# A graph layer's last normalisation moved into TensorE's products, with every third residual sum on ScalarE and GpSimd

## The chip, the cores and the metric

The kernel runs on one core of one Trainium2 chip. The metric is the device time of one execution in microseconds (us). Three executions of the kernel before took 1694.15, 1694.95 and 1696.44 us; their median is 1694.95 us.

## What is computed

A graph convolution layer on 6250 nodes with 256 channels and 100,000 edges, then a feed-forward layer with 8 experts of which each node takes one. Cut to the part that matters here, the end of the graph layer and what comes right behind it:

```python
edge_index = jnp.stack([src, dst])
# inside the graph layer, x is the layernorm of the input
h = _gcn_conv(x, W1, row, col, n_nodes)
h = jax.nn.relu(_batchnorm(h, g1, b1))
h = _gcn_conv(h, W2, row, col, n_nodes)      # 256 channels
h = _batchnorm(h, g2, b2)                    # per channel: h * a2 + b2
out = jax.nn.relu(h + res)                   # res = x
# around it
x = x + _L0_gnn_ref(_layernorm(x, axis=-1), edge_index, ...)
x = x + _L0_ffn_ref(_layernorm(x, axis=-1)[None], ...)[0]
```

So each node's row becomes x + relu(h * a2 + b2 + layernorm(x)), and that row is normalised once more (mean and variance over 256 channels) for the feed-forward layer.

## The kernel before, in words

The work goes through stages one after the other: edges are sorted into one-hot matrices, the first aggregation, the two linear maps, the second aggregation (to 1209 us of the profile), the end of the graph layer (`finish_gnn`), the gate with the hidden units (`gate`), and the experts. The change touches `finish_gnn` alone. It has no barrier to the gate: its five functions (`sync`, `gpsimd`, `vector`, `scalar`, `tensor`) are the first part of each engine's program in the gate's block, and each engine works in the order in which its instructions are written.

The nodes are cut into 49 tiles of 128 rows. Two tiles are a pair (25 pairs, the last with one tile) and four a group (13 groups, the last with one tile). A pair fills one of four PSUM banks, `m.ps[:, g % 4]`. The second convolution lies in `m.agg2` with the channels on the partitions, in two halves (KC = 2), so a tile has to be turned.

- SP (`sync`, L1563 and L1566) loads, for each group, 512 KB of x into `xr` and 512 KB of the stored layernorm(x), as two f16 parts, into `xnr`. Both are rings of 12 tiles, that is three groups. Group q + 3 is loaded once both pairs of group q have been summed (`s_x1`, L1571).
- DVE first makes the per-channel factors a2 and b2 (L1593 to L1602, the power on GpSimd at L1583).
- ScalarE (`affine`, L1662) applies a2 and b2 to `m.agg2` in place, two instructions of 128x512 for a group. It does four groups ahead, and then in turn: `normalise(q)` (L1669, four instructions of 128x256) and `affine(q + 4)`.
- TensorE (L1693, L1695) makes, for each tile, the sum in PSUM: two products of the identity with the f16 parts (256 columns each), then two fp32 products that turn the two halves of `m.agg2` by the identity `m.id32`. Each fp32 product is two instructions in the trace. It waits for the load, for the bank (`s_x1` of the pair four before) and for `s_v`, that is `affine` of the group. After the pairs 16 and 18 it turns the first two normalised pairs for the gate (L2024).
- DVE (`residual`, L1611) takes the pair out of PSUM: max with 0 plus x, to `m.rows`, 128x512. `stats` (L1619) takes the statistics of the pair before, and at the end of a group come L1625 and L1627; GpSimd raises to the power -0.5 (L1587), and `shifts(q)` (L1639) runs in DVE's step g = 2q + 4. So in a step DVE does residual(g), stats(g - 1), and in every second one the end of a group and a shift. In step 22 it does the gate's L2164 twice, in step 23 the gate's weights (L1631 to L1633).
- ScalarE's `normalise(q)` waits for that shift. Behind the last one it loads the table of Gelu and starts the gate (L2106).

## Time and profile before

| | |
|---|---|
| median of 3 executions | 1694.95 us |
| profiled execution, its own time | 1694.88 us |
| its span, first to last instruction | 1693.2 us |
| mean granted TensorE clock | 0.978 of full speed |
| `finish_gnn`, from SP's first load to TensorE's first hidden unit | 1209.42 to 1264.30 us |
| first Gelu of the gate | 1271.32 us |

The page of the profile gives busy shares over the whole span, which mix eight stages with different limits. For this change only the stretch from 1209 to 1272 us is read, by four views: the busy time of each engine in a stretch, the chain of work that ended last in order of time, the timeline of the instructions, and the groups of instructions by line with the time of one.

### The profile page before, as it was taken

The page shows a single profiled execution, that of the slowest core. Times are in us where ns is not written, and L with a number is a line of the kernel's source. Part 1 is how long each engine was busy: PE and PEld are TensorE (multiplying, and loading weights), DVE is VectorE, ACT ScalarE, POOL GpSimd, SP SyncE. Part 2 cuts the span into 40 slices and gives each one's busy share as a digit, 9 for nine tenths or more (in the row PEclk, how much of TensorE's full clock was granted, in tenths as well). Part 3 has the DMA queues.
Part 4 walks back from the last instruction along what each step waited for, and adds up shares of the span by engine and source line. Part 5 has one row for each costly group of instructions (what it writes and reads, how often), then busy time and mean ns, then how long its engine had stood idle before and what let it go on. Part 6 is the DMA issues. An engine that isn't in the chain of part 4 may idle for free. (4 is left out here: it accounts for less than half of the span.)

```text
span 1693.2 us, 32733 instructions
## 1 busy us (share of the span) xinstructions
PE 1473.3 (87%) x10003; PEld 1028.2 (61%) x10004; DVE 1091.2 (64%) x3900; ACT 851.7 (50%) x1611; POOL 1036.8 (61%) x1139
## 2 busy tenths in 40 slices
PE   0137999999999989798999999999779999839998
PEld 0114666666666669796665555556566666627776
DVE  6578888888888737683233343433386778767775
ACT  0555555555555535574234432221288877725665
POOL 5745677777777710244777777777223566637776
PEclk9999999999999999899999999999899999959999
DMA  7727666666666620046989999998489433489993
GB/s 242 203 90 258 200 201 208 203 206 211 200 209 210 203 61 0 23 163 230 324 286 313 316 311 324 329 324 277 139 279 343 162 152 151 164 212 262 271 271 87
DMA packets 219570, 364.80 MB, mean 215 GB/s; under 512 B 31416, under 2 KB 146551, under 8 KB 219174
## 3 DMA queue, kind: packets, MB, share of 16 engines
q1 hardware_dynamic: 158202, 217.62, 39.2%
q0 software_dynamic: 46816, 131.61, 24.7%
q10 hardware_dynamic: 14412, 13.86, 3.2%
q8 instruction: 69, 1.13, 0.3%
q14 instruction: 71, 0.58, 0.1%
HBM read 240.34 MB, written 130.12 MB: 219 GB/s over the span
## 5 line engine op out<-in xcount | busy, mean ns | idle before, releaser
L1181 POOL DMA_INDIRECT grows<-table_dram,gsrc x680 | 656.4, 965 | 248.3 <-issue 214.9
L1113 PE MATMUL ps<-table,adj 128*128 128x512 f16 x2842 | 705.0, 380 | 4.2 <-PEq L1330 4.2
L1113 PEld LDWEIGHTS ps<-table,adj 128*128 128x128 f16 x2842 | 389.5, 142 | 165.1 <-issue 6.8
L857 ACT ACTIVATE adj<-ps 128x490 f16<-128x490 f32 (+1 forms) x390 | 223.9, 574 | 179.5 <-PE ps L842 174.8
L829 DVE TENSOR_SCALAR oh_k<-iota_k,keyrem 128x246 f16<-128x246 f16 x780 | 237.1, 308 | 0.0
L828 DVE TENSOR_SCALAR oh_r<-iota_r,keyrem 128x128 f16<-128x128 f16 x780 | 211.9, 273 | 4.1 <-ACT keyrem L352 3.7
L1062 PE MATMUL ps<-grows,oh_g 128*128 128x512 f16 x680 | 166.5, 379 | 18.1 <-DMA grows<-table_dram,gsrc 17.8
L2395 PE MATMUL ps<-wd,h_hi 128*128 x896 | 152.7, 276 | 15.3 <-DVE h_lo L2443 15.3
L842 PE MATMUL ps<-oh_k,oh_r 128*128 128x245 f16 x780 | 148.8, 273 | 17.3 <-DVE oh_k L829 13.6
L842 PEld LDWEIGHTS ps<-oh_k,oh_r 128*128 128x128 f16 x780 | 75.7, 99 | 95.1 <-DVE oh_k L829 19.9
L934 DVE SCALAR_TENSOR_TENSOR tmp_d<-ps,disP,tmp_d 128x256 f32<-128x256 f32 x30 | 14.5, 484 | 183.6 <-ACT tmp_d L1140 183.6
L927 DVE TENSOR_SCALAR oh_g<-iota_r,gloc 128x128 f16<-128x128 f16 x680 | 124.8, 277 | 0.3 <-DVE cv_raw L806 0.2
L2395 PE MATMUL ps<-wd,h_lo 128*128 x448 | 123.2, 275 | 0.0
L1062 PEld LDWEIGHTS ps<-grows,oh_g 128*128 128x128 f16 x680 | 64.7, 98 | 94.9 <-DMA grows<-table_dram,gsrc 27.6
L2038 PE MATMUL ps<-q_xt_hi,fw_parts 128*128 128x512 f16 (+1 forms) x416 | 102.4, 368 | 5.0 <-DVE wg L1633 3.1
L1148 ACT ACTIVATE agg<-ps 128x256 f32<-128x256 f32 x98 | 37.4, 382 | 135.7 <-PE ps L1074 104.9
L2395 PEld LDWEIGHTS ps<-wd,h_hi 128*128 128x128 f16 x896 | 84.4, 99 | 32.2 <-issue 15.6
L2375 POOL DMA_INDIRECT out<-out_rows,token x56 | 75.4, 1346 | 46.5 <-POOL out_rows L2372 40.7
L2106 ACT ACTIVATE q_hf<-ps,b1f,unscale 128x512 f32<-128x512 f32 (+1 forms) x104 | 78.4, 754 | 41.2 <-PE ps L2038 37.9
L2175 DVE SCALAR_TENSOR_TENSOR q_h_lo<-q_hf,beta,q_h_hi 128x512 f16<-128x512 f32 (+1 forms) x104 | 74.6, 718 | 36.3 <-ACT q_h_hi L2117 34.4
L1140 ACT ACTIVATE tmp_d<-ps,disP 128x256 f32<-128x256 f32 x30 | 14.2, 474 | 159.8 <-PE ps L1113 159.8
L2443 DVE TENSOR_TENSOR h_lo<-back,h_hi 128x1024 f16<-128x1024 f32 x56 | 68.9, 1230 | 39.6 <-ACT h_hi L2412 39.5
(379 smaller groups left out, 2709.4 us busy)
## 6 DMA issues: line engine op xcount, KB each, us to landing
kept<-sorted_h SPq DMA_DIRECT2D x224, 128.0 KB
adj_dram<-adj SPq DMA_DIRECT2D x60, 367.5 KB
adj<-adj_dram SPq DMA_DIRECT2D x56, 367.5 KB, 7.5
cv_raw<-fwd SPq DMA_DIRECT2D x64, 256.0 KB, 6.7
adj_dram<-adj SPq DMA_DIRECT2D x30, 477.8 KB
adj<-adj_dram SPq DMA_DIRECT2D x28, 477.8 KB, 5.5
table_dram<-table SPq DMA_DIRECT2D x13, 896.0 KB, 4.1
grows<-table_dram,gsrc POOLq DMA_INDIRECT x680
```

What stands on the lines that cost most here:

```text
L828: dve.tensor_scalar(a.oh_r[:, n % OHR, i, :], m.iota_r[:, :], m.keyrem[:, 1, j, w:w + 1], None, ALU.is_equal)
L829: last = dve.tensor_scalar(a.oh_k[:, n % OHR, i, :], m.iota_k[:, :], m.keyrem[:, 0, j, w:w + 1], None, ALU.is_equal)
L842: last = pe.matmul(m.ps[:, n % 3, at:at + keys], a.oh_r[:, n % OHR, i, :], a.oh_k[:, n % OHR, i, 0:keys], start=True, stop=True)
L857: act.activation(m.adj[:, q % 3, d0:d0 + wide, :].rearrange("r d c -> r (d c)"), m.ps[:, n % 3, 0:wide * NT], ACT.Copy).then_inc(a.s_adj, 1)
L927: last = dve.tensor_scalar(m.oh_g[:, n % GOR, j, :], m.iota_r[:, :], m.gloc[:, g, part * BT + j:part * BT + j + 1], None, ALU.is_equal)
L1062: last = pe.matmul(acc, m.oh_g[:, n % GOR, j, :], m.grows[:, n % GR, j, :], start=False, stop=part == PT - 1 and j == PARTS[part] - 1)
L1113: last = pe.matmul(acc, adj[:, :, c], table[:, c, :], start=c == 0, stop=c == NT - 1)
L1181: pool.indirect_dma_start(m.grows[:, n % GR, j, :], None, m.table_dram, bass.IndirectOffsetOnAxis(ap=m.gsrc[:, g, part * BT + j:part * BT ...
L2038: last = pe.matmul(m.ps[:, c % UB, 0:wide], m.w1[:, 2 * k + half, w, at:at + P], x[:, i % 2, k, 0:wide], start=q == 0 and k == 0, stop=q = ...
L2106: act.activation(hf[:, c % HFR, 0:wide], m.ps[:, c % UB, 0:wide], ACT.Gelu, bias=m.b1f[:, h:h + 1], scale=m.unscale[:, 0:1]).then_inc(s_ge ...
L2375: pool.indirect_dma_start(a.out, bass.IndirectOffsetOnAxis(ap=token[:, q:q + 1], axis=0), outt[:, q % HB, :], None, bounds_check=N - 1, oo ...
L2395: last = pe.matmul(acc, h[:, q % HB, c, :], w[:, c // 2, half, c % 2, :], start=False, stop=h is h_lo and c == KH - 1)
```

## The change

- ScalarE no longer applies a2 and b2. DVE makes two diagonal matrices of a2 (`dg`), and TensorE turns with `dg[:, h, :]` in place of `m.id32`, so that the turned tile is scaled.
- b2 is added by one more product: a matrix `two` of 1/32 (64x128, float32r) with `shift2` (64x256, float32r), which holds a high part of b2's row in 32 partitions and the rest in the other 32. To get b2 as a row, DVE first fills `dg` with diagonals of b2, TensorE sums them over the partitions with `m.ones` into bank 7, and DVE copies that (64x256) and subtracts to get the rest. One wait `s_v` stands before the shift product of pair 0.
- The products are issued for a pair: two of 512 columns in place of four of 256, and one shift product of 512 columns.
- In the pairs 2, 5, 8, 11, 14, 17 and 20 (`aside`) the sum isn't DVE's: ScalarE takes the relu out of PSUM (`bare`, 128x512), GpSimd adds x (`add`, 128x512 fp32) and signals `s_added`. `stats` of such a pair, and the reload of its ring slot, wait for `s_added`; TensorE waits for `s_bare` before it uses the bank again. ScalarE does bare(g) for g in 2q + 4 and 2q + 5 before normalise(q); GpSimd does add(g) for g in 2q + 2 and 2q + 3 before the power of group q.

```diff
@@ -1549,11 +1549,20 @@
     s_ve, s_mh, s_rs, s_aff, s_v, s_sum = (S("g_" + n) for n in ("ve", "mh", "rs", "aff", "v", "sum"))
     s_h, s_x1, s_ve3, s_rs3, s_shift3, s_wg = (S("g_" + n) for n in ("h", "x1", "ve3", "rs3", "shift3", "wg"))
     s_in = [S(f"g_in{q}") for q in range(RG)]
+    s_bare, s_added = S("g_bare"), S("g_added")
     pairs = [(2 * g, min(2, NT - 2 * g)) for g in range(-(-NT // 2))]
     groups = [(GT * q, min(GT, NT - GT * q)) for q in range(-(-NT // GT))]
     done = [-(-(t0 + k) // 2) for t0, k in groups]
+    aside = [g for g in range(2, len(pairs) - 3, 3)]
+    shared = lambda n: sum(g < n for g in aside)
+    own = lambda n: n - shared(n)
     gw = m.gw
     m.s_normed = S("g_normed")
+    dg = take("dg", [P, KC, P], F32)
+    shift2 = take("shift2", [64, C], F32R)
+    two = take("two", [64, P], F32R)
+    s_wide = S("g_wide")
+    WIDE = 7
     assert take.next <= m.work + 6144
     def sync(sp):
         def load(q):
@@ -1568,7 +1577,9 @@
         for q in range(RG):
             load(q)
         for q in range(len(groups) - RG):
-            sp.wait_ge(s_x1, done[q])
+            sp.wait_ge(s_x1, own(done[q]))
+            if shared(done[q]):
+                sp.wait_ge(s_added, shared(done[q]))
             load(q + RG)
             if q == 3:
                 sp.dma_start(gw.wg_raw[:, :, :], a.fwg.rearrange("(k p) e -> p k e", p=P)).then_inc(gw.s_par, 16)
@@ -1581,8 +1592,21 @@
         pool.wait_ge(s_mh, 1)
         pool.wait_ge(s_ve, 1)
         pool.tensor_tensor(rs2[:, :], ve2[:, :], mh[:, :KC], ALU.pow).then_inc(s_rs, 1)
+
+        def add(g):
+            t0, k = pairs[g]
+            q = t0 // GT
+            at = t0 % RT
+            v = m.rows[:, t0:t0 + k, 0:C]
+            pool.wait_ge(s_in[q % RG], 32 * (q // RG + 1))
+            pool.wait_ge(s_bare, shared(g) + 1)
+            pool.tensor_tensor(v, v, xr[:, at:at + k, :], ALU.add).then_inc(s_added, 1)
+
         for q, (t0, k) in enumerate(groups):
             t = slice(t0, t0 + k)
+            for g in range(2 * q + 2 if q else 0, 2 * q + 4):
+                if g in aside:
+                    add(g)
             pool.wait_ge(s_ve3, q + 1)
             pool.tensor_tensor(rs3[:, t], ve3[:, t], mh[:, t], ALU.pow).then_inc(s_rs3, 1)
             if q in beside:
@@ -1599,10 +1623,22 @@
         dve.wait_ge(s_rs, 1)
         link(dve.tensor_tensor(a2[:, :], m.bn_g2[:, :], rs2[:, :], ALU.mult))
         link(dve.tensor_tensor(tmp[:, :], mv2[:, :, 0], a2[:, :], ALU.mult))
-        dve.tensor_tensor(b2[:, :], m.bn_b2[:, :], tmp[:, :], ALU.subtract).then_inc(s_aff, 1)
+        link(dve.tensor_tensor(b2[:, :], m.bn_b2[:, :], tmp[:, :], ALU.subtract))
+        for h in range(KC):
+            last = dve.tensor_scalar(dg[:, h, :], m.id32[:, :], b2[:, h:h + 1], None, ALU.mult)
+        last.then_inc(s_aff, 1)
+        dve.tensor_scalar(two[:, :], m.ones[0:64, :], 1.0 / 32, None, ALU.mult)
+        dve.wait_ge(s_wide, 1)
+        for h in range(KC):
+            dve.tensor_scalar(dg[:, h, :], m.id32[:, :], a2[:, h:h + 1], None, ALU.mult)
+        low = slice(32, 64)
+        link(dve.tensor_copy(shift2[:, :], m.ps[0:64, WIDE, 0:C]))
+        dve.tensor_tensor(shift2[low, :], m.ps[low, WIDE, 0:C], shift2[low, :].bitcast(F32), ALU.subtract).then_inc(s_v, 1)
 
         def residual(g):
 
+            if g in aside:
+                return
             t0, k = pairs[g]
             q = t0 // GT
             at = t0 % RT
@@ -1614,7 +1650,10 @@
         def stats(g):
             t0, k = pairs[g]
             q = t0 // GT
-            dve.wait_ge(s_x1, g + 1)
+            if g in aside:
+                dve.wait_ge(s_added, shared(g) + 1)
+            else:
+                dve.wait_ge(s_x1, own(g) + 1)
             for i in range(t0, t0 + k):
                 dve.bn_stats(st3[:, i, :], m.rows[:, i, 0:C]).then_inc(s_sum, 1)
             if t0 + k == sum(groups[q]):
@@ -1655,51 +1694,56 @@
         dve.tensor_copy(m.rows[:, :, C + 2], mv3[:, :, 0])
 
     def scalar(act, beside):
-        def affine(q):
-            t0, k = groups[q]
-            for h in range(KC):
-                v = m.agg2[:, h, t0 * P:(t0 + k) * P]
-                last = act.activation(v, v, ACT.Identity, bias=b2[:, h:h + 1], scale=a2[:, h:h + 1])
-            last.then_inc(s_v, 1)
-
         def normalise(q):
             t0, k = groups[q]
             act.wait_ge(s_shift3, q + 1)
             for i in range(t0, t0 + k):
                 act.activation(m.rows[:, i, 0:C], m.rows[:, i, 0:C], ACT.Identity, bias=shift3[:, i:i + 1], scale=rs3[:, i:i + 1]).then_inc(m.s_normed, 1)
 
-        act.wait_ge(s_aff, 1)
-        AHEAD = 4
-        for q in range(AHEAD):
-            affine(q)
+        def bare(g):
+            t0, k = pairs[g]
+            act.wait_ge(s_h, g + 1)
+            act.activation(m.rows[:, t0:t0 + k, 0:C], m.ps[:, g % 4, 0:k * C].rearrange("p (t c) -> p t c", c=C), ACT.Relu).then_inc(s_bare, 1)
+
         for q in range(len(groups)):
+            for g in range(2 * q + 4 if q else 0, 2 * q + 6):
+                if g in aside:
+                    bare(g)
             normalise(q)
             if q in beside:
                 beside[q]()
-            if q + AHEAD < len(groups):
-                affine(q + AHEAD)
 
     def tensor(pe, beside):
+        pe.wait_ge(s_aff, 1)
+        for h in range(KC):
+            last = pe.matmul(m.ps[:, WIDE, h * P:(h + 1) * P], m.ones[:, :], dg[:, h, :], start=True, stop=True)
+        last.then_inc(s_wide, 1)
         for g, (t0, k) in enumerate(pairs):
             q = t0 // GT
             if t0 % GT == 0:
                 pe.wait_ge(s_in[q % RG], 32 * (q // RG + 1))
             if g >= 4:
-                pe.wait_ge(s_x1, g - 3)
-            pe.wait_ge(s_v, q + 1)
+                pe.wait_ge(s_x1, own(g - 3))
+                if shared(g - 3):
+                    pe.wait_ge(s_bare, shared(g - 3))
+            at = t0 % RT
+            for n in range(2):
+                pe.matmul(m.ps[:, g % 4, 0:k * C], m.id16[:, :], xnr[:, at:at + k, n * C:(n + 1) * C], start=n == 0, stop=False)
+            if g == 0:
+                pe.wait_ge(s_v, 1)
+            pe.matmul(m.ps[:, g % 4, 0:k * C], two[:, :], shift2[:, :].unsqueeze(1).to_broadcast([64, k, C]), start=False, stop=False)
             for i in range(k):
                 acc = m.ps[:, g % 4, i * C:(i + 1) * C]
-                for n in range(2):
-                    pe.matmul(acc, m.id16[:, :], xnr[:, (t0 + i) % RT, n * C:(n + 1) * C], start=n == 0, stop=False)
                 for h in range(KC):
-                    last = pe.matmul(acc[:, h * P:(h + 1) * P], m.agg2[:, h, (t0 + i) * P:(t0 + i + 1) * P], m.id32[:, :],
-                                     start=False, stop=h == KC - 1)
+                    last = pe.matmul(acc[:, h * P:(h + 1) * P], m.agg2[:, h, (t0 + i) * P:(t0 + i + 1) * P], dg[:, h, :],
+                                     start=False, stop=i == k - 1 and h == KC - 1)
             last.then_inc(s_h, 1)
             if g in beside:
                 beside[g]()
         pe.wait_ge(s_wg, 1)
         pe.wait_ge(gw.s_w1, 16)
-        pe.wait_ge(s_x1, len(pairs))
+        pe.wait_ge(s_x1, own(len(pairs)))
+        pe.wait_ge(s_added, len(aside))
 
     lead = Names()
     lead.sync, lead.gpsimd, lead.vector, lead.scalar, lead.tensor = sync, gpsimd, vector, scalar, tensor
```

## Rows read from the trace of the kernel before

**Rows 1.** Busy time by stretch: us, each engine's busy time, clock, DMA share, GB/s.
```profile
1236.00:1246.00 10.00, 7.34 (x65) 6.65 (x64) 9.08 (x35) 9.65 (x18) 2.77 (x3) 1.00 0.89 281
```
**Rows 2.** Chain that ended last, in order of time: start us, us, what.
```profile
1234.33 0.16 DVE shift L1639
1234.52 2.07 ACT rows L1669 x4
1236.59 1.42 ACT agg L1662 x2
...
1239.74 0.69 DVE rows L1611
...
1241.12 0.39 DVE mv L1625 x4
1241.61 0.16 DVE shift L1639
...
1258.65 0.69 DVE rows L1611
...
1265.47 4.53 ACT rows L1669 x9
```
**Rows 3.** Timeline, start of the stage: start, us, engine, line, what.
```profile
1214.26 0.16 DVE L1602 TENSOR_TENSOR b2c<-bn_b,tmp 128x2 f32<-128x2 f32 x1
...
1216.49 1.06 PE L1695 MATMUL ps<-id,agg 128*128 128x128 f32 x4
...
1218.95 0.69 DVE L1611 SCALAR_TENSOR_TENSOR rows<-ps,x_ring 128x512 f32<-128x512 f32 x1 [4.53 <-PE ps L1695]
```
**Rows 4.** Timeline, TensorE, one tile at full clock, and the next tile.
```profile
1238.80 0.38 PE L1693 MATMUL ps<-xn_ring,id 128*128 128x256 f16 x2
...
1239.47 0.38 PE L1693 MATMUL ps<-xn_ring,id 128*128 128x256 f16 x2
```
**Rows 5.** Chain in the gate's stage: six f16 products of 512 columns.
```profile
1277.89 1.31 PE ps L2038 x6
```
**Rows 6.** Timeline, linear stage, TensorE: float32r products of 256 columns, start to start.
```profile
721.77 0.64 PE L1530 MATMUL ps<-w_hi,h_hi 128*128 128x256 f32 x4
722.25 0.64 PE L1530 MATMUL ps<-w_lo,h_hi 128*128 128x256 f32 x4
```
**Rows 7.** One line: the float32r product of 64 rows, 256 columns, durations.
```profile
L2391 PE MATMUL ps<-bd_rows,ones_r x56: 375/380/572, 1495.7 to 1683.9; 64*128 x56
```
**Rows 8.** Groups by line: busy us, mean ns: GpSimd adds of two widths, ScalarE's evacuation.
```profile
L2372 POOL TENSOR_TENSOR out_rows<-part_rows,x_rows 128x256 f32<-128x256 f32 x56 | 42.2, 754 | 17.3 <-ACT part_rows L2423 17.1
...
L1348 POOL TENSOR_TENSOR w_lo<-w_raw,w_hi 128x1024 fp32r<-128x1024 f32 x1 | 2.4, 2367 | 0.1
...
L2125 ACT ACTIVATE turned<-ps x52: 277/587/599, 1278.0 to 1484.9; 128x512 f32<-128x512 f32 x48, 128x128 f32<-128x128 f32 x4
```
**Rows 9.** Issue of one group's loads, and the landing of single loads of xn_ring.
```profile
1238.57 0.37 SPq L1563 DMA_DIRECT2D x_ring<-x  x1
1238.98 0.51 SPq L1566 DMA_DIRECT2D xn_ring<-xn_dram  x1
...
DMA to landing us min/median/max: 4.9/4.9/4.9
...
DMA to landing us min/median/max: 6.0/6.0/6.0
```
**Rows 10.** Groups by line, DVE: small operations like those added.
```profile
L2275 DVE TENSOR_SCALAR bd_parts<-bd,g_up 64x256 fp32r<-64x256 f32 x1 | 0.3, 345 | 0.0
```
**Rows 11.** Timeline, linear stage: DVE with and without GpSimd beside it.
```profile
727.97 0.68 DVE L1422 TENSOR_TENSOR h_lo<-h_all,h_hi 128x512 fp32r<-128x512 f32 x1
...
728.97 1.29 POOL L1361 CAST h_hi<-h_all 128x512 fp32r x2 [1.30 <-ACT h_all L1474]
729.33 0.48 DVE L1426 SCALAR_TENSOR_TENSOR table<-ps,dis,table 128x256 f32 x1 [0.69 <-ACT table L1479]
729.73 1.06 DVE L1422 TENSOR_TENSOR h_lo<-h_all,h_hi 128x512 fp32r<-128x512 f32 x1
```

## The prediction, made before the changed kernel was run

> **What bounds the kernel now.** I read the busy times by stretch first. In ten steady microseconds of the stage ScalarE is busy for 9.65 us, DVE for 9.08 and TensorE for 7.34 [rows 1]. Two engines are close to full and neither is quite, so I went to the chain of work in order of time. It shows a circle: a shift on DVE at 1234.33, four instructions of normalise (2.07 us), two of affine (1.42), a pair on TensorE, the residual at 1239.74, statistics, the end of a group, and the shift two groups on at 1241.61 [rows 2]. That circle of 7.28 us carries four pairs: 1.82 us a pair. ScalarE's own work in it is 2 x (2.07 + 1.42) = 7.0 us, so ScalarE is nearly the bound and the waits around it are the rest. The last part matters as well: residual(22) starts at 1258.65, and what follows it (steps 22 to 24 on DVE, nine instructions of normalise for 4.53 us, Gelu's table) leads to the first Gelu [rows 2]. From there the gate and the experts run as they did. So the time is the profiled 1694.88 us plus the shift of residual(22). The profiled execution stands 0.07 us under the median of 1694.95.
>
> **What goes.** The 26 instructions of affine leave ScalarE, 2 x 0.71 us a group by the chain [rows 2], some 17 us in all, and with them the circle. Seven of 25 residuals leave DVE. Every remaining product has to be made by engines that had slack, so the question is what is late next.
>
> **The start.** b2 is ready at 1214.26 + 0.16 = 1214.4 [rows 3]. Before, affine of group 0 followed, and residual(0) started at 1218.95 [rows 3]. Now two diagonals of 128x128 come first. No row has just that; the nearest is 0.345 us for 64x256 [rows 10], the half of it is 0.17 for 128 columns, and I take 0.2 each (bounds 0.1 and 0.35): 1214.9. TensorE's two fp32 sums are four instructions at half clock, 1.06 us for four [rows 3]: 1216.0. DVE then makes two diagonals (0.4), the copy of 64x256 (0.35), and the subtraction (0.35 to 0.5) [rows 10]: about 1217.3. TensorE's two f16 products are done by then. The shift product and eight fp32 instructions at half clock are twice 0.24 and twice 0.88 (below), 2.2 us, and with 0.2 to the signal pair 0 is complete at 1219.7. So residual(0) starts 0.75 us later than it did. After that I let TensorE run at full clock, as before, where it had risen to it by then.
>
> **TensorE for a pair.** Before: a tile takes 1239.47 - 1238.80 = 0.67 us, 0.22 for the two f16 products and 0.45 for four fp32 instructions [rows 4], so 1.33 a pair. Now: two f16 products of 512 columns, 1.31 / 6 = 0.218 each [rows 5]; eight fp32 instructions, the same form as before, 0.88; and the shift product. Four float32r products of 256 columns start 0.48 apart [rows 6], 0.12 each, so 0.24 for 512 columns. The one with 64 rows shows 0.380 us from start to end [rows 7], which holds its fill and its weights; twice that less nothing is the upper bound, 0.76, and 0.11 (half of an f16 one) the lower. I take 0.24, since [rows 6] are a dense stream, as this is. Sum: 0.44 + 0.24 + 0.88 = 1.55 us a pair, 0.22 more than before. TensorE alone, from pair 0 at 1219.7, would complete pair 22 after 22 x 1.55 + 0.9 for the gate's turned pairs, at 1254.7. That is 4 us before 1258.65: TensorE isn't the bound yet.
>
> **DVE.** From the residual at 1239.74 to the end of its step's statistics at 1241.12 are 1.38 us, and a group's end with the shift takes 0.49 to 0.65 more [rows 2]. Four pairs without waiting cost 4 x 1.38 + 2 x 0.57 = 6.7 of the 7.28 us. With a third of the residuals gone, each 0.69 [rows 2], it is (6.7 - 0.9) / 4 = 1.45 a pair: under TensorE's 1.55. DVE isn't the bound either, whatever the sums aside save it.
>
> **The path through a pair that is put aside.** ScalarE takes the relu out of PSUM: 0.587 us for 128x512 [rows 8]. GpSimd's add of 128x512 has no row. The nearest are 0.754 us for 256 columns and 2.367 for 1024 [rows 8]; between them 512 columns lie at 1.29, which I take, with 0.75 and 2.37 as ends. So a pair put aside is summed about 0.1 + 0.59 + 1.29 = 2.0 us after TensorE, where DVE needs 0.7. Its statistics stand one step later on DVE, 1.55 + 0.69 = 2.2 us after, so they just fit. But its ring slot also comes free later. For the pairs 5, 11 and 17, each the second of its group, SP's wait on `s_added` is what releases the group three on; behind it SP's queue holds all later loads.
>
> **The loop that decides.** From add(5) to add(11): issue of x, 0.03 + 0.41 us until that of xn; its landing, in six steady loads 4.9 three times, then 5.0, 5.8 and 6.0, mean 5.25 (the ends in [rows 9]); pairs 10 and 11 on TensorE, 3.10 and 0.2 to the signal; relu 0.59; add 1.29. Sum 10.87 us for six pairs: 1.81 a pair, where the old circle had 1.82 [rows 2]. The removed bound is replaced by an equal one. Placing it: pair 5 completes at 1219.7 + 5 x 1.55 = 1227.45; add(5) ends at 1229.4; two laps give 1251.1 for add(17). Then issue 0.44, landing 5.25, pair 22 at 1.55, signal 0.2: residual(22) can start at 1258.6, against 1258.65. The sum is a change of 0.0 us, and 1695.0 us.
>
> Its ends: landing always 4.9 makes three loads 1.0 us faster, always 6.0 makes them 2.3 slower (the DMA share is already 0.89 [rows 1], so crowded loads are likelier than free ones); the add at 0.75 gives -1.6, at 2.37 gives +3.2 (three adds in the chain); the shift product at 0.76 would add 0.5 to each of ten pairs, +5, at 0.11 takes 1.3 off; the diagonals' bounds move the start by -0.4 to +0.6. Two extremes at once in the same direction are unlikely. SP's load of the hidden units' weights stands behind these waits too, but it moves with them by under 2 us, and TensorE waits for DVE's L1633 then.
>
> Is the add a risk to DVE? While GpSimd's cast ran, DVE's instruction with two SBUF inputs took 1.06 us in place of 0.68, and the one that reads PSUM kept its 0.48 [rows 11]. DVE's residual reads PSUM and one ring, the statistics one tensor, so I cost the sharing at nothing; if each of seven adds cost DVE 0.38, that is 2.7 us in an engine with slack, under 1 at the end. The Trainium skill (GPSIMD Engine Reference, 1. Specifications) says that GpSimd's SBUF interface is shared with VectorE, with contention for instructions that have two SBUF inputs or use a two-port mode: by that rule the residual is spared too, and the trace agrees with it. The same page (3.1 Elementwise) calls GpSimd the wrong engine for plain elementwise work and gives 2.6 cycles an element at 1.2 GHz, an estimate of 1.11 us for this add; with it the sum would be 0.5 us lower.
>
> **The rivals.**
> 1. The loads don't hold the stage. If the landings stay at 4.9 us and the add is nearer to 1.0, the chain drops under TensorE's own pace. Then TensorE and DVE in their order set it: residual(22) between 1254.7 (TensorE alone) and about 1255.5 with DVE's waits, so 3.2 to 4.0 us gained: 1691.3. For it: the transfers have gaps, share 0.89. Against: TensorE's waits are then all gone, which needs every load on time. Chance 0.13.
> 2. Slower: the ring slot's late release. If the add takes over 1.9 us beside DVE's traffic, or loads that are issued closer together than before land in 6.0, each lap grows by 1.0 to 1.4 us and nothing gives it back: 3 x 1.3 = +4, 1699. It decides from a lap over 12.0 us. For it: the DMA share, and that two of the six landings were near 6. Against: the narrow add's 0.754 was steady in 56 of them. Chance 0.15.
> 3. The change doesn't do what it says: the shift product isn't cheap (0.76), so TensorE takes 2.07 a pair and is the bound from start to end: 1219.7 + 22 x 2.07 + 0.9 = 1266.1, 7.5 us later: 1702.5. Only the isolated product [rows 7] speaks for it, the dense stream against it [rows 6]. Chance 0.03.
>
> **How the numbers follow.** The forecast, no change within the spread of landings, has 0.69. A measurement here tells apart about 0.2%, 3.4 us. Rival 1 lies at that bound, so 0.11 of its chance and of the forecast's low tail counts as faster; rival 2 and 3 give 0.17 slower; 0.72 within. The range leaves out a tenth on each side: 1691.8 to 1698.8.
>
> **What would show it right or wrong.** Right: no L1662; TensorE's pairs 1.55 apart when it doesn't wait; it waits for the loads of groups 5, 8 and 11, over 1 us each; SP's longest waits end by GpSimd's add; add(11) to add(17) near 10.9 us; ScalarE under 75% busy. Wrong: if TensorE waits for nothing between pairs 6 and 22 (rival 1), if the adds take over 1.9 us or the lap over 12 (rival 2), if pairs on TensorE are 2 us apart (rival 3), or if the first Gelu moves otherwise than residual(22) does.

## The result, and the profile of the changed kernel

| | before | after |
|---|---|---|
| median of six executions each | 1694.55 us (1691.45 to 1696.44) | 1701.03 us (1699.92 to 1702.71) |
| ratio, 95% interval | | 1.0041 (1.0031 to 1.0051) |
| profiled execution, its own time | 1694.88 us | 1700.47 us |
| mean granted TensorE clock | 0.978 | 0.976 |
| first load of the stage to residual(0) | 9.53 us | 11.04 us |
| first load to residual(22) | 49.23 us | 56.54 us |
| first load to first Gelu | 61.90 us | 69.20 us |
| first Gelu to the end of the span | 421.9 us | 421.6 us |

The changed kernel is 6.5 us slower, outside the forecast range (1691.8 to 1698.8). The table's lower half is read from the timelines: the whole loss stands before residual(22), 1.5 us in the start and 5.8 us in the 22 pairs between, and the first Gelu moved with it (+7.3). Behind the first Gelu the two agree within 0.3 us. The two spans differ by less, 5.4 us (1698.6 and 1693.2), because the changed kernel's profile reached this stage 1.6 us sooner, by stages that the change doesn't touch. So the question is about 46 us of this one stage. The marks come from one profile each; they are finer than whole times, since executions of one kernel differ by 2 or 3 us elsewhere.

The busy times of the ten microseconds that answer to [rows 1] (columns as there):

```profile
1236.00:1246.00 10.00, 9.67 (x56) 6.33 (x55) 6.32 (x30) 5.12 (x11) 4.49 (x4) 1.00 0.82 245
```

ScalarE fell from 9.65 to 5.12 and DVE from 9.08 to 6.32, as meant. TensorE rose from 7.34 to 9.67: it is the bound. From 1237.9 us to the residual of pair 22 the chain of work in order of time has nothing else in it (start us, us, what):

```profile
1232.36 5.51 DMA xn_ring<-xn_dram
...
1247.82 0.43 PE ps L1731 x2
1248.25 0.42 PE ps L1734
1248.67 1.09 PE ps L1738 x8
1249.76 0.43 PE ps L1731 x2
...
1263.17 1.10 PE ps L1738 x8
...
1264.36 0.69 DVE rows L1647
```

A pair takes 1249.76 - 1247.82 = 1.94 us where the forecast had 1.55. The timeline of TensorE and of its weight loads (PEld) shows where it goes; the brackets hold the idle time ahead of a row:

```profile
1227.70 0.59 PE L1731 MATMUL ps<-xn_ring,id 128*128 128x512 f16 x2
1228.22 0.50 PE L1734 MATMUL ps<-shift,two 64*128 64x512 f32 x1
1228.65 1.16 PE L1738 MATMUL ps<-dg,agg 128*128 128x128 f32 x8
1229.65 0.60 PE L1731 MATMUL ps<-xn_ring,id 128*128 128x512 f16 x2
...
1228.22 0.18 PEld L1734 LDWEIGHTS ps<-shift,two 64*128 64x128 f32 x1 [0.42 <-issue]
1228.65 0.97 PEld L1738 LDWEIGHTS ps<-dg,agg 128*128 128x128 f32 x8 [0.25 <-issue]
```

From start to start: 0.52 us for the two f16 products, 0.43 for the shift product, 1.00 for the eight fp32 instructions, 1.95 in all. The load of the 64-row weights starts at the very moment of its product, 1228.22, after 0.42 us in which the loader did nothing, and the load of the next 128-row weights starts with its product too, after 0.25 us. The waits by reason, from 1216 to 1264 us, say the same of the whole stage (total us, times, longest):

```profile
DVE rows L1647 <- PE ps L1738: 17.1, 13, 3.0
PEld ps L1734 <- issue: 9.7, 22, 0.8
PEld ps L1738 <- issue: 6.0, 23, 0.4
PE ps L1731 <- DMA xn_ring<-xn_dram: 0.3, 1, 0.3
```

DVE waits for TensorE 13 times, and TensorE waits for a load once, for 0.3 us. That is the load of group 5 at the head of the chain above; the relu and the add of pair 5 released it. So the loop on which the forecast rested is touched once and costs 0.3 us; it doesn't set the pace.

The start of the stage, in the timeline:

```profile
1212.85 0.48 DVE L1628 TENSOR_SCALAR dg<-id,b2c 128x128 f32<-128x128 f32 x2
1213.38 1.22 PE L1719 MATMUL ps<-dg,ones 128*128 128x128 f32 x4 [7.64 <-DVE dg L1628]
1215.48 0.42 DVE L1636 TENSOR_TENSOR shift<-ps,shift 32x256 fp32r<-32x256 f32 x1
1216.68 2.08 PE L1738 MATMUL ps<-dg,agg 128*128 128x128 f32 x8
1218.54 1.06 PE L1731 MATMUL ps<-xn_ring,id 128*128 128x512 f16 x2
...
1221.86 0.59 PE L1731 MATMUL ps<-xn_ring,id 128*128 128x512 f16 x2
```

Pair 1 runs from 1218.54 to 1221.86, 3.32 us, nearly all of it at half clock (the lower of the clock's two levels, 1.2 GHz): in the busy times by stretch TensorE's granted clock is 0.50 from 1219 to 1221, 11.2 to 13.2 us behind the first load, and 0.86 in the next two. Before, it was 0.85 already 9.6 to 11.6 us behind it.

With that the loss closes. Between residual(0) and residual(22) lie 22 pairs at 1.945 (42.8), 1.38 more for pair 1, two turned pairs of the gate at 0.44 (0.9) and 0.3 of waiting: 45.4, and the trace has 56.54 - 11.04 = 45.5.

### The profile page after: what moved, and what is told of

It reads as the page before. It is cut to its first block and busy times, and to the rows that moved or that the text cites. A ratio compares the mean times of both kernels' runs of the same rounds, so it can differ in the third digit from the quotient of the medians.

```text
span 1698.6 us, 32690 instructions
## 1 busy us (share of the span) xinstructions
PE 1491.4 (88%) x9984; PEld 1029.7 (61%) x9985; DVE 1088.3 (64%) x3900; ACT 837.3 (49%) x1592; POOL 1044.4 (61%) x1146
## 3 DMA queue, kind: packets, MB, share of 16 engines
q8 instruction: 68, 1.11, 0.3%
```

## The experiments

The theory before the first run was that the shift product's 64 rows cost, or its type, or both; the rivals were the sums put aside and the products for pairs. The short marks below are us behind the stage's first load. The chips of e5, e6, e8 and e9 took some 2000 us for every kernel, those of e9b, e6b, e10 and e7 some 1974. There the stage began at 1470 to 1502 us instead of 1206 to 1210. Its own rows agree: e5's stage repeats that of the changed kernel, and the stored layernorm's loads land after 4.8 to 5.8 us in e7 and 4.9 to 6.0 in before. So the marks of all runs are set side by side. How finely they can be read is shown by e3, e6, e6b, e9 to e12 and e14 to e16, which run the same instructions up to pair 1: their residual(1) lies anywhere from 11.85 to 13.02 us, since the clock rises at another moment in each, 11.0 us behind the first load in e3 and 11.7 in e15. Differences of about 1 us between two rows are therefore not read as effects.

| run | residual(0) | residual(22) | first Gelu | median, and kernel before on the same chip | ratio (95%) |
|---|---|---|---|---|---|
| before | 9.53 | 49.23 | 61.90 | | |
| after | 11.04 | 56.54 | 69.20 | 1701.03 / 1694.55 | 1.0041 (1.0031 to 1.0051) |
| e1 float32r, 128 rows | 10.76 | 50.86 | 63.52 | 1699.70 / 1694.35 | 1.0034 (1.0021 to 1.0047) |
| e2 f16, 64 rows | 10.87 | 53.71 | 66.37 | 1698.54 / 1694.35 | 1.0029 (1.0019 to 1.0038) |
| e3 f16, 128 rows | 10.58 | 50.59 | 63.24 | 1695.88 / 1694.35 | 1.0009 (1.0001 to 1.0018) |
| e4 no shift product | 10.33 | 49.93 | 62.59 | 1697.10 / 1694.35 | 1.0011 (1.0000 to 1.0022) |
| e5 after, no pair aside | 11.06 | 56.48 | 69.13 | 2011.3 / 2003.94 | 1.0051 (1.0021 to 1.0082) |
| e6 e3, no pair aside | 10.57 | 49.05 | 61.70 | 2003.93 / 2003.94 | 1.0009 (0.9985 to 1.0033) |
| e6b the same | 10.58 | 49.48 | 62.12 | 1974.33 / 1973.74 | 0.9987 (0.9952 to 1.0022) |
| e8 before, pairs aside | 9.53 | 52.52 | 65.17 | 2009.82 / 2003.94 | 1.0023 (0.9996 to 1.0051) |
| e7 before, products for pairs | 9.53 | 49.94 | 62.60 | 1975.85 / 1973.74 | 1.0006 (0.9981 to 1.0031) |
| e9 e3, first pair of five groups aside | 10.59 | 52.30 | 64.95 | 2000.88 / 2003.94 | 0.9994 (0.9969 to 1.0018) |
| e9b the same | 10.58 | 52.50 | 65.14 | 1971.87 / 1973.74 | 0.9990 (0.9956 to 1.0024) |
| e10 e3, first pair of ten groups aside | 10.58 | 52.44 | 65.07 | 1977.91 / 1973.74 | 1.0017 (0.9979 to 1.0054) |
| e11 e3, half-height loads | 10.57 | 50.95 | 63.62 | 1695.60 / 1694.71 | 1.0008 (0.9994 to 1.0023) |
| e14 e9, half-height loads | 10.38 | 49.41 | 62.05 | 1695.23 / 1694.71 | 1.0002 (0.9992 to 1.0011) |
| e12 e6, half-height loads | 10.31 | 49.77 | 62.42 | 1694.85 / 1694.71 | 1.0003 (0.9993 to 1.0013) |
| e13 before, half-height loads | 9.52 | 50.86 | 63.53 | 1694.61 / 1694.71 | 1.0001 (0.9991 to 1.0010) |
| e15 e3, x alone loaded | 10.58 | 47.50 | 60.14 | 1691.88 / 1693.91 | 0.9989 (0.9979 to 0.9998) |
| e16 e9, x alone loaded | 10.45 | 47.71 | 60.35 | 1692.34 / 1693.91 | 0.9990 (0.9980 to 0.9999) |

**Height and type of the shift product (e1, e2, e3).** e1 fills both operands to 128 rows, the upper half of `two` with zeros; e2 keeps 64 rows in f16; e3 does both.

```diff
-    shift2 = take("shift2", [64, C], F32R)
-    two = take("two", [64, P], F32R)
+    shift2 = take("shift2", [P, C], F32R)      # e2: [64, C], F16; e3: [P, C], F16
+    two = take("two", [P, P], F32R)            # e2: [64, P], F16; e3: [P, P], F16
...
+        dve.tensor_scalar(two[64:P, :], m.ones[64:P, :], 0.0, None, ALU.mult)   # e1, e3
```

> The changed kernel with a shift product of 128 rows in place of 64: the two matrices get 128 partitions, the lower 64 rows of the weights are zero. Same type (float32r), same columns, same sum. Theory height: the trace of the changed kernel shows TensorE's pairs 1.94 us apart, not 1.55, and before the 64-row weights and again before the 128-row weights behind them the weight load starts only when the product before has nearly ended; a change of the rows in use stops the load from running ahead. Then here the pairs that don't wait are 1.55 to 1.62 us apart, and the loop of load, relu and add that I had predicted sets the pace: 1694 to 1697 us. Theory type: float32r of 512 columns, or its 4-byte weights, costs 0.43 us as such. Then the pairs stay at 1.9 and the time at 1701.

> The changed kernel with the shift product in f16 (high part and rest of b2's row in f16, weights f16), still of 64 rows. Theory height: nothing is gained, pairs 1.85 to 1.95 us apart, 1700 to 1701 us. Theory type: pairs at 1.55 to 1.6, and 1694 to 1697 us.

> The changed kernel with the shift product in f16 and of 128 rows. Both theories expect pairs of 1.52 to 1.58 us. What it tells: my prediction's loop (load of a ring slot, two pairs, relu on ScalarE, add on GpSimd: 1.81 us a pair) as the next bound expects 1694 to 1697 us, with TensorE waiting over 1 us for the loads of groups 5, 8 and 11. If TensorE's pace is all that matters, 22 pairs at 1.53 in place of 1.94 give 9 us: 1692.

Height is the cause. With 128 rows residual(22) comes at 50.86 and 50.59, with 64 rows at 56.54 and 53.71. The type is worth 2.8 us with 64 rows, and with 128 rows 0.3, which can't be told from nothing. Some of this is the clock's: residual(1) follows residual(0) by 3.27 us in the changed kernel, 2.20 in e1, 2.45 in e2 and 1.87 in e3, and whether the height delays the clock's rise or only its scatter shows here stays open. A pair of e1 on TensorE, and the load of the same weights:

```profile
1254.31 0.60 PE L1732 MATMUL ps<-xn_ring,id 128*128 128x512 f16 x2 [0.59 <-DMA xn_ring<-xn_dram]
1254.57 0.58 PE L1735 MATMUL ps<-shift,two 128*128 128x512 f32 x1
1254.98 1.05 PE L1739 MATMUL ps<-dg,agg 128*128 128x128 f32 x8
1255.88 0.59 PE L1732 MATMUL ps<-xn_ring,id 128*128 128x512 f16 x2
...
1254.54 0.19 PEld L1735 LDWEIGHTS ps<-shift,two 128*128 128x128 f32 x1
```

The pair takes 1255.88 - 1254.31 = 1.57 us, and the weights' row has no idle time ahead of it any more. The f16 product of 64 rows in e2 still has both idle times:

```profile
1253.00 0.39 PE L1734 MATMUL ps<-shift,two 64*128 64x512 f16 x1
1253.32 1.16 PE L1738 MATMUL ps<-dg,agg 128*128 128x128 f32 x8
...
1254.84 0.09 PEld L1734 LDWEIGHTS ps<-shift,two 64*128 64x128 f16 x1 [0.42 <-issue]
1255.16 0.97 PEld L1738 LDWEIGHTS ps<-dg,agg 128*128 128x128 f32 x8 [0.23 <-issue]
```

Its pair takes 1.84. What the type still saves is the exposed load itself, 0.09 us against 0.18. So in these traces the weights of 64 rows aren't loaded while products of 128 rows run, nor the other way round, and each change of height lays the end of one product and the next load bare: 1.94 - 1.57 = 0.37 us a pair in float32r, 1.84 - 1.54 = 0.30 in f16 (e3's pairs stand 1.54 apart).

The Trainium skill (TensorEngine Tiling (Array Packing), Key Properties) says that a change of tiling mode, not just of the tile, drains TensorE. The idle 0.42 and 0.25 us would agree with that, if a plain product of 64 rows is such a change; whether it is this rule that acts, no run here shows.

In whole times the height shows between e2 (1.0019 to 1.0038) and e3 (1.0001 to 1.0018), not between the changed kernel and e1. e1's five executions spread from 1695.83 to 1702.00 us, and their median, 1699.70, misses the 1694 to 1697 that were expected. Its profile is that of the lowest, so the marks speak for that one; why others took longer is open. e2 took 1698.54 us and 1.84 a pair, where the height alone was expected to leave 1700 to 1701 and 1.85 to 1.95; e3's time came as expected.

**The price in place (e4).** The shift product is left out, so b2 is missing from the sum.

```diff
-            pe.matmul(m.ps[:, g % 4, 0:k * C], two[:, :], shift2[:, :].unsqueeze(1).to_broadcast([64, k, C]), start=False, stop=False)
```

> The changed kernel without the shift product in the pairs; b2's row is still made, but not added, so that part of the computation is missing. TensorE's pair would take 0.44 + 0.88 = 1.32 us. The predicted loop without the shift product is (0.44 + 5.25 + 2.64 + 0.2 + 0.59 + 1.27) / 6 = 1.73 us a pair, 1693 to 1695 us. If the loads land in time whatever the pace, DVE's 1.45 a pair is the bound: 1690 to 1691. Its difference to the changed kernel is the whole price of the shift product where it stands: 6 to 8 us by the loop, 10 by DVE.

The shift product of the changed kernel cost 69.20 - 62.59 = 6.6 us at the first Gelu, as the loop had it (6 to 8); that of e3 only 0.65, less than the marks can tell. So in e3 TensorE's work isn't the bound any more. The medians show less: 1701.03 against 1697.10, 3.9 us, and e4's misses its expected 1693 to 1695. Its executions spread from 1691.7 to 1700.0, with 1694.65 for the profiled one.

**The sums put aside (e5, e6, e8).** e5 takes them out of the changed kernel and e6 out of e3; e8 adds them alone to the kernel before, where ScalarE still applies a2 and b2.

```diff
-    aside = [g for g in range(2, len(pairs) - 3, 3)]
+    aside = []
...
-        pe.wait_ge(s_added, len(aside))
```

> The changed kernel (shift product float32r of 64 rows) with no pair put aside: DVE takes all 25 residuals, ScalarE and GpSimd sum none. If TensorE's 1.94 us a pair is the bound in the changed kernel, the third of the sums on other engines neither helps nor harms: DVE needs 1.67 a pair, residual(22) starts within 0.5 us of where it did after the stage's start (56.5 us) and the time is 1700 to 1702. If the pairs put aside were what slowed the changed kernel, it would be 1696 to 1698.

> The f16 shift product of 128 rows, and no pair put aside. DVE's work without waiting is 1.67 us a pair, the ring's loop without relu and add (0.44 + 5.25 + 3.1 + 0.2 + 0.7) / 6 = 1.61, TensorE 1.55. If the late release of ring slots through add(5), add(11) and add(17) holds the kernel with this product and pairs aside (its residual(22) starts 50.6 us after the stage's start, with 3.6 us of waits for loads), this one is faster by 22 x 0.1 to 0.14 = 2 to 3 us at that point, at 47.5 to 48.5, and the time 1692 to 1694. If not, it is slower, since DVE has more to do.

> The kernel before with one part of the change alone: the pairs 2, 5, 8, ... 20 summed by ScalarE and GpSimd; a2 and b2 are still applied by ScalarE. ScalarE's work becomes 2 x 3.49 + 1.33 x 0.59 = 7.8 us for four pairs, over the circle's 7.28, and relu stands ahead of normalise and affine in its order: 1.94 us a pair, residual(22) 2 to 4 us later, 1697 to 1698. By the other view (DVE's work is the bound, ScalarE's waits are slack) it would be 2 us faster.

Under the 64-row product the sums do nothing: 56.48 without and 56.54 with them. Behind e3 they cost 1.1 to 1.5 us. On the kernel before they cost 3.3. Its chain there:

```profile
1532.40 0.07 DVE shift L1663
1532.50 2.08 ACT rows L1693 x4
1534.58 1.41 ACT agg L1686 x2
1535.99 1.97 ACT rows L1693 x4
1537.95 1.41 ACT agg L1686 x2
1539.36 0.49 ACT rows L1698
...
1539.99 1.29 POOL rows L1598
...
1543.92 0.07 DVE shift L1663
```

Normalise, affine and the relu (L1698) stand behind one another without a gap, and the add and the statistics behind them, up to the next shift: 11.52 us from shift to shift for six pairs, 1.92 a pair where the old circle had 1.82 and 1.94 was expected. So the relu and the add have both entered the circle. e6 missed its expectation, 47.5 to 48.5, by 0.6 us, and e6b, the same kernel, lies 1.0 above it; they come back to the old 49.23 and no further.

**What bounds e3.** With the price gone, the loop of the forecast is there, in its own order:

```profile
1226.75 1.29 POOL rows L1603
...
1228.10 0.37 SPq L1572
...
1228.52 5.75 DMA xn_ring<-xn_dram
...
1234.32 0.60 PE ps L1732 x2
...
1237.60 0.61 ACT rows L1707
...
1238.34 1.28 POOL rows L1603
...
1240.10 4.89 DMA xn_ring<-xn_dram
```

From the end of add(5), 1228.04, to the end of add(11), 1239.62, it is 11.6 us for six pairs, where the forecast had 10.87; the landing was 5.75 instead of 5.25, and the two pairs, the first after a wait, 3.26 instead of 3.10. The next lap, to the end of add(17) at 1250.78, took 11.2. TensorE waits 1.62, 1.06 and 0.72 us for the loads of groups 5, 8 and 11, where over 1 us each was expected.

**Other pairs aside (e9, e9b, e10).** If the late release by the second pair of a group holds the loop, taking the first pair of a group aside should free it.

```diff
-    aside = [g for g in range(2, len(pairs) - 3, 3)]
+    aside = [g for g in range(2, len(pairs) - 3, 4)]      # e10: step 2
```

> The f16 shift product of 128 rows, with the pairs 2, 6, 10, 14 and 18 put aside in place of 2, 5, 8, ... 20: all of them the first pair of their group, so that a ring slot is released by DVE's residual of the second pair. By the loop theory the release is no longer late: (0.44 + 5.25 + 3.1 + 0.2 + 0.7) / 6 = 1.61 us a pair, DVE 1.49, TensorE 1.55: residual(22) at 46.5 to 48 us after the stage's start, 1690.5 to 1693. If the place of the pairs in their groups doesn't matter, it stays near 50, 1695.

> The kernel of e9 once more, on another chip, since all kernels there took 2000 us with longer stages before this one. Loop theory: residual(22) at 46.5 to 48 us after the stage's start. The first look had 49.1 with a gap of 5 us between two residuals; if that gap comes again, the theory lacks something.

> The kernel of e6 (f16 shift product of 128 rows, no pair put aside) once more on another chip. The first Gelu came 61.7 us after the stage's start there, against 63.2 with the pairs put aside (e3). Loop theory: again 61 to 62 us, and a time of 1693 to 1695. If the other chip had disturbed the stage, it would lie elsewhere.

> The f16 shift product of 128 rows, and the first pair of every group put aside (2, 4, ... 20: ten pairs). DVE's work is 1.32 us a pair, the ring's release stays with DVE: loop 1.61, TensorE 1.55. Loop theory: as e9b within 0.5 us, the relief of DVE brings nothing more. If DVE's work were the bound in e9b, this one would be 1 to 3 us earlier.

All three came out at 52.3 to 52.5, later than e3, where earlier was expected; e6b's first Gelu, at 62.12, was about as expected. The timeline of e9b shows a late load and what it brought:

```profile
1518.84 0.60 PE L1732 MATMUL ps<-xn_ring,id 128*128 128x512 f16 x2 [2.18 <-DMA xn_ring<-xn_dram]
...
1519.50 1.83 PE L1739 MATMUL ps<-dg,agg 128*128 128x128 f32 x8
1521.12 1.06 PE L2069 MATMUL ps<-id,rows 128*128 128x128 f32 x4
1521.97 1.06 PE L1732 MATMUL ps<-xn_ring,id 128*128 128x512 f16 x2
```

and its busy time by stretch:

```profile
1518.00:1522.00 4.00, 3.16 (x16) 2.84 (x17) 1.32 (x3) 0.77 (x2) 1.05 (x2) 0.70 1.01 333
```

One load, issued while the share of the DMA engines' time stood at 0.95 to 1.10, landed after 7.4 us. TensorE waited 2.18 us for it, and soon after that idle time its granted clock fell to the lower of its two levels: eight fp32 instructions took 1.83 us instead of 1.05, the f16 pair of products 1.06 instead of 0.60, and the clock's mean over 1518 to 1522 is 0.70. The same instructions, from that load to the first fp32 one of the next pair, took 4.29 us here (to 1523.13) and 2.63 in e3 (1245.04 to 1247.67). So 1.7 us are the clock's, nearly all of the 1.9 by which e9b is later than e3. The waits aren't longer in sum, 3.3 us for loads against e3's 3.6, but two of them make it up. e9 and e10 show the same, a fall of the clock behind waits of 2.12 and 2.53 us. The length of the wait doesn't decide it alone: behind 2.64 us in e4 and 2.06 in e8 the clock stayed up.

**The transfers (e11 to e16).** Two ways of taking bytes away. In e11 to e14 only 64 of the 128 partitions of `xnr` are loaded from group 3 on; the other rows are stale. In e15 and e16 the stored layernorm isn't loaded again, but for the last group, and x comes in two halves to keep the count of the semaphore, so the bytes are halved over all partitions. The lines are cut:

```diff
+            rows = P if q < RG else P // 2                  # e11 to e14
+                sp.dma_start(xr[:, at + b:at + b + 2, :], ...).then_inc(s_in[q % RG], 16)   # e15, e16: b = 0 and 2, no xnr
```

> The kernel of e3 (f16 shift product of 128 rows, every third pair aside) with less to load: from group 3 on only 64 of the 128 partitions of the stored layernorm are loaded, 256 KB in place of 512, so half of these rows of the sum are stale and that part of the computation is wrong. TensorE, DVE, ScalarE and GpSimd do the same instructions. In e3 the stage loses 3.6 us in waits for loads. Loop theory: landing about 0.9 us earlier, three of them in the chain: residual(22) 2.5 to 3.5 us earlier than in e3 (50.6 after the stage's start), at 47 to 48. If only the late release by relu and add mattered and not the transfer, it would stay at 50 or above.

> The kernel of e9 (first pairs of groups aside) with the same halved load. In e9 the loads landed up to 7.4 us after their issue, at a DMA share of 0.96, and residual(22) came at 52.4. Transfer theory: the DMA queue was full; now landings are back at 4 to 5 us and residual(22) comes at 46 to 47.5, earlier than in any kernel so far. If something else in the order of this kernel holds it (a wait of statistics for the add), it stays over 50.

> The kernel of e6 (f16 shift product of 128 rows, no pair aside) with the halved load. Its residual(22) came at 49.1 and 49.5 with 2 us of waits for loads. If DVE's 1.67 us a pair is its bound, it gains those waits at most: 47 to 48.5. If the transfer is, as in e14: 46 to 47.

> The kernel before with the halved load. My reading of its chain is that ScalarE's circle of normalise and affine sets the pace and the loads are in time: residual(22) stays within 0.5 us of 49.2. If the load is the hidden bound of the kernel before too, it comes 2 us earlier.

None of the four came where it was expected (e11 only where it would stay if the transfer didn't matter), and they settle little. Half the bytes over half the partitions landed no sooner: 5.41, 5.63 and 6.61 us in e11's chain against 4.89, 4.93 and 5.75 in e3's, and the kernel before got 1.6 us later by it. Only e14 says something: where e9's clock fell its own stays at 1.00, and residual(22) comes 2.9 us earlier, of which some 1.7 are the clock's, going by e9b.

> The kernel of e3 with the stored layernorm loaded for the first three groups and the last only; the other groups load x alone, in two transfers of 256 KB over all 128 partitions, and TensorE adds a stale layernorm, which is the part of the computation that is wrong. The load over 64 partitions (e11) landed 5.4 to 6.6 us after its issue, no sooner than a full one, so e11 didn't test the transfer; this does. Transfer theory: landing 3.5 to 4.2 us after the first issue in place of 5.3 to 6.7, so the loop is (0.03 + 4 + 3.1 + 0.2 + 0.59 + 1.27) / 6 = 1.53 us a pair, no more than TensorE's 1.54: residual(22) 45.5 to 47.5 us after the stage's start, in place of 50.6. If the late release by relu and add is the whole of it, 50 to 51 again.

> The kernel of e9 (first pairs of groups 2, 6, ... 18 aside) with the loads of e15. Transfer theory: residual(22) at 45 to 47, within 1 us of e15, though these two lay 1.8 us apart with full loads (50.6 and 52.4); both are then at TensorE's pace (10.6 + 22 x 1.54 + 0.9 = 45.4). If e16 stays over 49, the place of the pairs aside has a cost of its own that isn't the transfer.

e15 came at 47.50, the upper end of what was expected. e16 missed its 45 to 47 with 47.71, but lies within the expected 1 us of e15. Busy times of e15, then of e16, in its steady stretch:

```profile
1223.00:1253.00 30.00, 29.44 (x215) 24.33 (x214) 27.22 (x104) 20.24 (x40) 16.62 (x15) 1.00 0.54 160
```
```profile
1225.00:1255.00 30.00, 29.41 (x212) 24.05 (x210) 25.14 (x97) 19.39 (x38) 14.66 (x14) 1.00 0.50 152
```

With a DMA share of 0.54 TensorE is busy for 29.44 of 30 us, from pair 1 on 18 of its 23 steps are 1.53 or 1.54 us, and residual(22) comes at 47.50, 3.1 us before e3's; e16 gains 4.8 on e9b, 1.7 of them the clock's, and ends at the same place. So the transfers hold e3 and e9. With them out of the way it makes no difference which pairs are put aside, at least at TensorE's pace, where both now stand. Whether one of the two orders would be the faster one ahead of a quicker TensorE, these runs can't show.

**The products for pairs (e7).** The kernel before, with the two f16 products of 512 columns alone.

```diff
-                for n in range(2):
-                    pe.matmul(acc, m.id16[:, :], xnr[:, (t0 + i) % RT, n * C:(n + 1) * C], start=n == 0, stop=False)
...
+            for n in range(2):
+                pe.matmul(m.ps[:, g % 4, 0:k * C], m.id16[:, :], xnr[:, at:at + k, n * C:(n + 1) * C], start=n == 0, stop=False)
```

> The kernel before with one part of the change alone: the f16 products issued for a pair, two of 512 columns in place of four of 256. TensorE isn't in the bound of the kernel before except for the two pairs of its circle, whose columns are the same. The first pair of a group completes no earlier. Expected: residual(22) within 0.3 us of 49.2 after the stage's start, and the time within 1 us of the kernel before.

residual(22) comes 0.7 us later, twice what was expected at most. TensorE's clock is still 0.50 from 9.3 to 11.3 us behind the first load, where that of before had a mean of 0.85 from 9.6 to 11.6. That is all of it: residual(1) is already 0.7 us late (12.01 against 11.28), and nothing is added behind it. Since kernels with the same start differ by more than this, it isn't shown to be the products' doing. In whole time the difference can't be told from nothing.

No version here that computes the whole sum is faster than the kernel before by its interval: the lowest ratio is e6b's, 0.9987 (0.9952 to 1.0022).

## Why the prediction was wrong, point by point

- **What bounds the kernel before.** Right as far as tested: in e8 the relu and the add lengthened the circle of [rows 2] from 1.82 to 1.92 us a pair, and residual(22) came 3.3 us later.
- **TensorE for a pair, the step that failed.** The shift product was taken at 0.24 us, from a dense stream of products with 128 rows [rows 6], and the row with its own number of rows [rows 7] was left as an upper bound. With 128 rows it is 0.22 in e3's chain. With 64 it takes 0.43 from its start to that of the fp32 instructions, and it costs 0.08 at the f16 products (0.52 where 0.44 was taken) and 0.12 at the fp32 instructions (1.00 for 0.88): 0.63 in all for 0.24. "Dense" was the wrong likeness; the height of the neighbours was the right one. The pair at 1.55 was right for the kernel that this one isn't: e15 has 1.54. The range has a second slip in the same term: it gave a shift product of 0.76 us +5, ten pairs with the loop still as the bound, while rival 3 had +7.5 at the same price, with TensorE as the bound in every pair. At the measured 1.94 a pair the loop's lap is 0.44 + 5.25 + 3.88 + 0.2 + 0.59 + 1.29 = 11.65 us and TensorE's six pairs are 11.64. The two bounds meet there, which fits the single wait of 0.3 us.
- **Rival 3, chance 0.03, is what happened.** It put 2.07 us a pair and 1702.5 us; measured were 1.94 and 1701.0. Its sign, "pairs 2 us apart", is in the trace. That it came within 1.5 us is in part luck: its price was twice a row's duration and not a change of height, and the 0.13 us too much in each of 22 pairs, 2.9 us, stood in for the 0.75 of the start and the 1.4 of the clock that it didn't have. The chance was too small: only one row was on its side, but that row was the only one with 64 rows.
- **The start.** Taken at +0.75 us, it was +1.5. The diagonals were 0.24 each (taken 0.2), the four fp32 instructions 1.22 (taken 1.06), the copy and the subtraction 0.41 and 0.42 (taken 0.35 and up to 0.5). From the first pair's shift product at 1215.95 to residual(0) at 1218.86 it was 2.9 us, where 2.4 were taken with the signal. Here the 64 rows count too, at half clock: e1 starts 0.3 us sooner and e3 0.5.
- **"After that I let TensorE run at full clock."** Wrong by 1.4 us in this trace: by the mean of 0.86 over 1221 to 1223 the clock rose near 1221.5, and pair 1 took 3.32 us.
- **The loop that decides.** It doesn't set the pace of the changed kernel; in e3 it appears as told, with laps of 11.6 and 11.2 instead of 10.9 us. They and a start of the first lap 0.6 us later leave residual(22) 1.4 us later than before, where 0.0 was forecast. That a nearly equal bound waits behind the removed one was right to within that.
- **Relu, add, DVE.** The relu took 0.59 us as taken. The add took 1.27 (taken 1.29, between 0.75 and 2.37), as the rows by line show:

```profile
L1603 POOL TENSOR_TENSOR rows<-rows,x_ring 128x512 f32<-128x512 f32 x7 | 8.9, 1270 | 29.2 <-ACT rows L1706 29.2
L1706 ACT ACTIVATE rows<-ps 128x512 f32<-128x512 f32 x7 | 4.1, 591 | 30.0 <-PE ps L1738 29.9
```

DVE's residual kept its time beside GpSimd. In e3's timeline one ran wholly under an add in 0.69 us, its time without one:

```profile
1232.60 1.27 POOL L1603 TENSOR_TENSOR rows<-rows,x_ring 128x512 f32<-128x512 f32 x1 [1.71 <-ACT rows L1707]
1232.80 0.69 DVE L1648 SCALAR_TENSOR_TENSOR rows<-ps,x_ring 128x512 f32<-128x512 f32 x1 [0.34 <-PE ps L1739]
```

The Trainium skill (GPSIMD Engine Reference, 3.1 Elementwise) gives 2.6 cycles an element, at 1.2 GHz an estimate of 1.11 us; the row has 1.27, so the interpolation between [rows 8] was the better source.
- **Rival 1** stayed shut for the reason given against it: the loads. Only without half of their bytes does residual(22) move before 49 us (47.50).
- **Rival 2** (laps over 12 us) didn't come by the add, which was short. The changed kernel's laps are over 12 us (12.2 and 12.1 from add(5) to add(11) to add(17)), but by TensorE's pace. Its other leg, crowded loads at 6 us and more, is what e9 and e10 ran into.

Left open: why e6 isn't earlier than before (DVE or the loads), why most of e1's executions took longer than its profile, and what makes the clock rise sooner or later at the start of the stage.

## What to carry to other kernels

Price an added product from a row with its own number of rows, and with neighbours of the height that it will have; where only the odd one differs, fill it with zero rows, which here brought a pair from 1.94 to 1.57 us. Where a term has wide bounds, ask at which value another engine becomes the bound, and let the range follow that one from there on. When a bound is removed, work out the next two before spending on a third engine: here 0.4 us a pair on TensorE was enough to make every saving on ScalarE and DVE idle. In these kernels a ring's release time and the bytes of a step set a floor that moving work between engines didn't lower.

## What was not expected of the hardware

- Between products of 128 and of 64 rows, the weights of the next aren't loaded under the running product: 0.42 and 0.25 us of idle loader a pair, none with 128 rows throughout.
- A float32r product of 512 columns and 128 rows is nearly as fast as an f16 one in a stream: 1.57 and 1.54 us a pair.
- Waits of 2.12, 2.18 and 2.53 us on TensorE (e9, e9b, e10) were each followed by some 3 us at the lower clock; waits of 1.62, 2.06 and 2.64 us (e3, e8, e4) weren't. By its length alone a wait couldn't be told to cost the clock.
- The same instructions at the start of the stage reached pair 1's residual at 11.85 to 13.02 us in eleven runs, by when the clock rose.
- Loads into 64 of 128 partitions with half the bytes landed after 4.9 to 6.6 us (e11), no sooner than the full ones, 4.9 to 6.3 (e3).
